# Leaving out the identity products that TensorE runs in its planned waits, in a four-stream transformer kernel

## The reference, cut to what matters

```python
x = x + tanh(g_xattn[0]) * L0_xattn(ctx, ctx, layernorm(x))      # linear feature map with exp, 16 heads
x = x + tanh(g_ffn[0])   * L0_ffn(layernorm(x))                  # butterfly stages around a gelu, 256 -> 1024 -> 256
x = x + tanh(g_xattn[1]) * L1_xattn(layernorm(x), ctx, ctx)      # softmax attention, masked by batch
x = x + tanh(g_ffn[1])   * L1_ffn(layernorm(x))                  # linear layer with two of 8 low-rank experts
x = x + tanh(g_xattn[2]) * L2_xattn(layernorm(x), ctx, ctx)
x = x + tanh(g_ffn[2])   * L2_ffn(layernorm(x))                  # quantised linear layers, gelu between them
x = x + tanh(g_xattn[3]) * L3_xattn(layernorm(x), ctx, ctx)      # masked by query and key
x = x + tanh(g_ffn[3])   * L3_ffn(layernorm(x))                  # gated silu layer with two of 8 experts
```

## Time and profile before

| | |
|---|---|
| median of three runs | 2626.75 us |
| lowest, highest run | 2623.39, 2628.63 us |
| profiled execution: span from first to last instruction | 2625.2 us |
| profiled execution: its own time | not recorded apart from the span; the median is 1.55 us above the span |
| PE (matmul) busy | 2472.9 us, 94% of the span, 21300 instructions |
| PE weight loads busy | 1670.9 us, 64% |
| DVE busy | 1491.8 us, 57% |
| ACT busy | 1204.5 us, 46% |
| POOL busy | 1170.3 us, 45% |
| bytes over HBM | 13 GB/s over the span |

### The profile page before, as it was taken

One profiled execution on the slowest core, in us unless ns is written; L12 is line 12 of the kernel. 1 busy time (PEld: TensorE's weight loads), 2 busy tenths in 40 slices (PEclk: granted clock), 3 DMA queues, 4 the chain that ended last, 5 costly groups with the idle time before them and its releaser, 6 DMA issues.

```text
span 2625.2 us, 53630 instructions
## 1 busy us (share of the span) xinstructions
PE 2472.9 (94%) x21300; PEld 1670.9 (64%) x21300; DVE 1491.8 (57%) x3948; ACT 1204.5 (46%) x1930; POOL 1170.3 (45%) x2521
## 2 busy tenths in 40 slices
PE   8999888999999988899999998899999999889998
PEld 5676445777776644577777655467767765447776
DVE  7555787545433687754543467874543257876442
ACT  5535477322244547723224546762322545674221
POOL 2334644545343554444533355444534345545442
PEclk9999999999999999999999999999999999999999
DMA  3200100000000000000000000000000000000000
GB/s 130 84 12 12 76 14 2 1 9 9 9 9 12 12 1 14 2 6 12 1 9 20 1 12 1 12 1 9 9 9 9 12 1 12 1 1 1 5 5 9
DMA packets 16279, 37.37 MB, mean 14 GB/s; under 512 B 1408, under 2 KB 11424, under 8 KB 15008
## 3 DMA queue, kind: packets, MB, share of 16 engines
q1 hardware_dynamic: 16032, 33.94, 3.7%
HBM read 29.74 MB, written 4.19 MB: 13 GB/s over the span
## 4 chain that ended last, share of the span: by engine, by line
PE 74%; DVE 14%; ACT 5%; POOL 4%; issue 3%; DMA 0%; DVEq 0%; POOLq 0%; ACTq 0%
PE P L1431 8%; PE P L1239 4%; PE P L1247 4%; PE P L1140 4%; PE P L1464 4%; PE P L1440 4%; PE P L1449 4%; PE P L1313 4%; PE P L1432 4%; PE P L1300 4%; PE P L1288 4%; PE P L1219 4%; DVE mx L1849 4%; ACT ET L1585 2%; PE P L1109 2%
## 5 line engine op out<-in xcount | busy, mean ns | idle before, releaser
L1849 DVE TENSOR_REDUCE mx<-P 128x8 f32<-128x1232 f32 x256 | 367.7, 1436 | 195.8 <-PE P L1136 63.5
L872 POOL TENSOR_SCALAR sm<-sm 128x1 f32<-128x1 f32 x512 | 174.6, 353 | 457.9 <-DVE sm L1845 457.4
L1431 PE MATMUL P<-xT,w 128*128 128x256 f32 x1024 | 265.6, 382 | 1.5 <-DVE sm L2042 0.8
L1543 ACT ACTIVATE xn<-x,sm 128x256 f32<-128x256 f32 x256 | 139.5, 593 | 228.3 <-POOL sm L878 228.2
L1885 DVE SCALAR_TENSOR_TENSOR x<-P,w_first,x 128x512 f32<-128x512 f32 x96 | 71.9, 749 | 290.7 <-PE P L1465 109.1
L1431 PEld LDWEIGHTS P<-xT,w 128*128 128x128 f32 x1024 | 190.3, 190 | 51.7 <-issue 25.9
L1585 ACT ACTIVATE ET<-P 128x2048 f32<-128x2048 f32 x96 | 180.1, 1876 | 68.1 <-PE P L1222 46.4
L1663 ACT ACTIVATE gu<-P 128x256 f32<-128x256 f32 x128 | 49.0, 383 | 331.1 <-PE P L1432 311.0
L1140 PE MATMUL P<-KB,R 32*128 32x308 f32 x1536 | 156.5, 476 | 39.0 <-ACT ET L1585 16.2
L2072 DVE SCALAR_TENSOR_TENSOR gu<-gu,P 128x256 f32<-128x256 f32 x128 | 53.7, 419 | 215.9 <-ACT gu L1663 215.6
L1219 PE MATMUL P<-R,KB 32*128 32x256 f32 x2048 | 162.3, 403 | 8.3 <-DVE mx L1849 8.3
(11 more groups left out here) (310 smaller groups left out, 5583.7 us busy)
## 6 DMA issues: line engine op xcount, KB each, us to landing
kvw<-in_wkv SPq DMA_DIRECT2D x12, 672.0 KB, 4.0
x<-in_x SPq DMA_DIRECT2D x16, 256.0 KB, 2.9
out<-x SPq DMA_DIRECT2D x16, 256.0 KB, 2.1
w<-in_w SPq DMA_DIRECT2D x2, 1024.0 KB, 6.3
w<-in_wexp SPq DMA_DIRECT2D x1, 1028.0 KB, 7.8
w_w<-in_wcon SPq DMA_DIRECT2D x1, 1024.0 KB, 10.1
w_w<-in_m3t SPq DMA_DIRECT2D x1, 1024.0 KB, 8.6
w<-in_w1q SPq DMA_DIRECT2D x1, 1024.0 KB, 10.6
```

The costliest lines, as they stand in the source:

```text
L872: own(e.tensor_scalar(a[:, i:i + 1], y[:, i:i + 1], y[:, i:i + 1], hv[:, i:i + 1], ALU.mult, ALU.mult), 1)
L1431: e.matmul(o, wm[:, c, js], s.xT[:, c, :], start=n == c == 0, stop=False, skip_group_check=True)
L1849: e.tensor_reduce(s.mx[:, i, :, 2 * u:2 * u + 2], quad[:, :, 0:2 * NK].rearrange("p g (a k) -> p g a k", a=2), AX.X, ALU.max).then_inc(q_d, 1)
```

## The change

The rule in `orders` that adds `fill` goes, and so does the function that played it. Nothing is put in its place.

```diff
@@ orders @@
                 if p[2] == "ACT":
                     p[3] += 1300.0 * (TABLE.get(p[1], table[0]) != table[0])
                     table[0] = TABLE.get(p[1], table[0])
-
-                if p[2] == "PE" and at - free["PE"] > 900.0 and let["bank"]:
-                    if let["bank"][0][0] < free["PE"] + 300.0:
-                        lists["PE"].append(("fill", let["bank"][0][1], int(0.6 * (at - free["PE"]) / 215.0)))
                 p[5] = at + p[3] + HOP[p[2]]
@@ pe_program @@
                 return P[:, k, :]
-
-            def fill(k, n):
-
-                o = take(k)
-                for _ in range(n):
-                    e.matmul(o, identb[:], identb[:].unsqueeze(1).broadcast_to([128, 4, 128]), start=True, stop=True)
@@
-            stages = {"fill": fill, "grow": grow, ...
+            stages = {"grow": grow, ...
```

More of the change, by code:

```diff
@@ L1467, in f3 @@
                 free[k] = [(s.d_x, X.up(s.d_x))]
-            stages = {"fill": fill, "grow": grow, "near": near, "upt": upt, "tsum": tsum, "key": key, "val": val,
+            stages = {"grow": grow, "near": near, "upt": upt, "tsum": tsum, "key": key, "val": val,
                       "turn": turn, "qp": qp, "sc": sc, "mt": mt, "st": st, "sts": sts, "s2": s2, "pv": pv, "pz": pz, "out": out_,
```

## The result

With the products left out the kernel takes 2647.06 us (median of four runs, 2644.68 to 2652.61). The kernel before takes 2625.97 us (2623.39 to 2628.63) with a fourth run added to its three. The ratio is 1.0082, with a 95% interval of 1.0067 to 1.0097. That is 21.1 us slower, where the forecast was 10 us slower: the direction and the range hold, but the effect is twice as large as the sum said.

The account below looks back on a forecast made before the run. The prediction took PE (TensorE) as the bound, with 74% of the chain. Its terms, -1.85 + 0 + 7.5 + 4.5 = +10.15 us on 2626.75, gave 2637 us, 0.4% slower, range 2624 to 2654.

Parts of the forecast that it names:

- Theory A: Set up for the experiments: the 24 added low-clock stretches are the whole loss, since the products kept the clock up.
- time lost in stretches at full clock: Sign named beforehand that the prediction is wrong: time lost where the clock is not low, which nothing in it explains.
- new low stretches: Term: half-clock stretches behind 23 lengthened pauses, three in four, at 1.25 or 0.4 us each: 7.5 + 4.5 us.
- 23 places: Pauses of 2.0 to 4.3 us without a matmul once products go, with no low stretch behind them before.
- 8 PE-bound places: Those of the 23 with the chain on PE throughout or nearly so: 8 x 3/4 x 1.25 = 7.5 us.
- The fifteen others: Those of the 23 with the chain mostly on DVE, POOL or ACT: 15 x 3/4 x 0.4 = 4.5 us.
- Savings: Products on the chain away from the opening, at 68.03, 399.08, 1039.80 and 1679.02: 1.85 us saved by their removal.
- The opening: Start of the kernel, 18 products at 4.47 and 11 later: between -1.7 and +2.5 us, taken as 0.
- Semaphore waits: A group's wait on its bank passes to the next step using that bank: 0.
- The clock holds: Rival: real matmuls around a wait keep the clock up, so the change is faster, about 2621 us; chance 0.12.
- Off the path: Rival: low stretches come but are mostly covered by waits for other engines: +2, 2629 us; chance 0.17.
- Every low stretch counts: Rival: PE's delay reaches the chain at all 23 places: 23 x 1.25 - 1.85 = +27, 2654 us; chance 0.15.

Follow-up runs that it names:

- e1: Changed kernel with the identity groups' bank waits kept in PE's list but no products, against the kernel before: 2644.97 us, ratio 1.0070.
- e2: Kernel before with only the 8 PE-bound groups (45 products) kept and the other 62 left out: 2639.44 us, ratio 1.0042.
- e3: Kernel before with only 15 groups (101 products) kept, those with the chain behind them on DVE, ACT or POOL: 2642.10 us, ratio 1.0059.
- e4: Kernel before without ten tight groups (27 products), and with 9 products in place of 18 at the opening: 2624.76 us, ratio 1.0000.
- e9: Kernel before without the opening's four groups (18, 4, 7 and 8 products): 2630.37 us, ratio 0.9999.

## Why the prediction was right in its sign and half in its size

**Right: the mechanism.** Theory A holds for the bulk of the loss: the products' absence lowers the clock (e1), and the time follows the clock, between kernels and between executions of one kernel. The clock fell to 0.977, just below the 0.978 to 0.985 that were named, with 24 more stretches where 12 to 20 were named. Over the fourteen kernels of the table the span goes with the number of low stretches, from 2614.9 us with 3 to 2644.9 with 36 (30.0 us for 33, 0.9 us each); all the others lie within 5.5 us of that line. But the prediction named "time lost in stretches at full clock" as a sign against it, and some was: 1.4 us at 760.58, and most of the 1.3 us left from the opening goes with a late load too. Without both, the 24 stretches cost about 17 of the 19.7 us, 0.7 us each.

**The term "new low stretches": right by place, too small by number.** Of the 23 places 17 got a low stretch, where 23 x 3/4 = 17.25 was forecast; what no row had suggested is that three of them, behind 2270.97 for one, got two in a row, so that it is 20 stretches. Of these, nine came behind seven of the 8 PE-bound places. I followed the lag of each step of PE behind the same step before; across these places it grew by 0.8, 2.5, 0, 1.5, 1.6, 2.6, 1.6 and 1.6 us, 12.1 us together instead of 7.5. The price was right (12.1 / 9 = 1.34 against 1.25), but not all of the reason given for it: weight loads don't double, yet in the changed kernel's trace one of 128x128 in f32 takes 0.33 us at the low clock (median) against 0.19 at full clock. At these eight the three quarters and the single stretch were too low.

**The fifteen others: priced too high in the lag, about right in the experiment.** The lag rose behind only one of them (8.5 to 10.9 us, the pair at 986.9), and fell by 1.3 to 1.7 us at the three that stand ahead of the bare wait of L1087 in the first three passes: there the new stretch took the place of the old one. Put back alone they gave 5.0 us (forecast 4.5). Why the two readings differ is not shown; that a group also protects its neighbours would do it, and 5.0 us is itself good only to some 3 us.

**The step that failed** lies in the count of new stretches, and the prediction did not write it down as a choice: that only places with 2.0 us or more without a matmul get new stretches, and all other groups are worth nothing. The 24 more stretches are 20 at the 23 places, one fewer behind the three old ones, and five more elsewhere (8 before, 13 after; some went and more came): behind a bare wait at 926.83 that had been harmless, at 304.2 and 1543.2, where one stretch became two, and in the last step of the kernel. The e2 and e3 runs leave some 8 us, good to some 3, to the groups that the forecast left out. The bare-wait rows were read one by one, from one execution, as if each wait decided for itself. The same 1.62 us with a fall in the changed kernel and without one in e1, where the same matmuls run, shows that it does not.

**Savings: 1.85 us forecast, 0.4 us seen.** The lag falls by 0.41 us at 68.03, as forecast. At 399.08 the pair is gone and the step behind it is 0.43 us earlier, but the scores after that now wait 0.35 us for ACT, so nothing comes back, nor at 1039.80 and 1679.02. That the tight groups are worth nothing agrees with e4, which can't tell less than some 3 us.

**The opening: 0, right.** e9 shows it alone at 0.9999. DVE's first statistics did not come near 12.0, as "what would show it" had said, but at 14.69 with everything out and at 13.20 with only the opening's groups out: the bound taken for the gain, the load of x, was the wrong one. The statistics stand behind a growth step in DVE's order, and the growth steps wait for their load until 8.42 to 9.92 us and then run slowly.

**Semaphore waits: 0, right** (e1).

**The rivals.** "The clock holds" fell: seven of the eight places lost it. "Off the path" is what happened at most of the fifteen, but not at the eight. "Every low stretch counts", at +27, came nearer than the forecast's +10 to the 21 us measured, with 24 stretches for its 23, but at 0.82 us instead of 1.25. The Trainium skill's rule in "TensorE: Matmul & The Clock Gate", section "Why this matters for your kernels", that long idle gaps between bursts should be avoided, had the right sign, and taken as certain gave +14, still too low. It speaks of long gaps; the trace agrees at most of the 23 places, but the fall at 928.80 stands behind a wait of 1.62 us.

What stays open: which waits are followed by a fall, place by place, since this differs even where the matmuls are the same; how much of the 24 is this execution's own; and what the closing stage is worth by itself.

## What to carry to other kernels

Identity products in TensorE's waits can be worth more than they look, and where they end before the releaser does, the chain shows no cost for them: here 296 of them bought 21 us, and 250 more in the right waits another 13. Put them where the trace shows waits, not where the planner believes in them, and look for them in the chain afterwards; when they stand there, they have become too many. When such work is judged, count the stretches at the low clock over the whole program and price them by what a stretch costs on the average (0.7 to 1.1 us in this kernel, by the way it is reckoned), instead of taking up each gap alone. Do it over several executions, because the count of one kernel moves by some stretches from one to the next, and look for lags that grow at full clock, which belong to something else.

## What the runs showed of the hardware that was not expected

- Behind the same bare wait of 1.6 us the clock fell to 0.50 in the changed kernel and stayed at 1.00 in the kernel before and in e1_waits_only, though the last has the changed kernel's matmuls in the same order. With five products and a wait of 1.8 us the clock stayed at 1.00 in the kernel before and fell to 0.50 in e2_eight.
- In 23 executions of one kernel on one chip the mean clock went from 0.989 to 0.995 and the time from 2634.63 to 2621.72 us.
- With one product in each wait there were 30 stretches, with half of the products 24, with none 36 and with all 12: the number of stretches went down step by step with the products.
- Some falls last twice as long: 6.8 us at 0.50, with PE busy for 5.62 us of it at 341.66 and for 6.13 us at 2270.30. Why some do and others don't is not shown.
- The same load of 256 KB let DVE start 2.6 us after its issue in one execution and 4.2 us after it in another, and PE's lag grew by 1.4 us behind it.
